# Hybrid attention, feed-forward and selective-scan kernel: the scan's per-tile work for the next tile in a new order, and three edits where stages meet

## The chip, the cores and the metric

The kernel runs on one core of a Trainium2 chip. The metric is the device time of one execution in microseconds (us). Three executions of the kernel before took 1989.69, 1992.88 and 1998.08 us; the median is 1992.88 us. The core's engines work side by side, each through its own list of instructions in order: TensorE (PE, with its weight loads as PEld), VectorE (DVE), ScalarE (ACT), GpSimd (POOL) and SyncE (SP), which issues the DMAs. They wait for each other by semaphores.

## What is computed

x is (4, 1024, 256) in float32, 4096 tokens. Four blocks follow each other, each on the layer-normed x and added to x:

```python
x = x + attn_a(_layernorm(x))   # 16 heads, latent q and kv, rotary part, softmax over 1024 keys
x = x + ffn(_layernorm(x))      # square(relu(x W_fc)) W_proj, 5 spiking steps
x = x + attn_b(_layernorm(x))   # selective scan, below
x = x + ffn(_layernorm(x))
```

The part that most of the change is in:

```python
x_res, z, params = x @ W_x.T, x @ W_z.T, x @ W_params.T
dt = softplus(params[..., :64] @ W_dt.T + b_dt)        # (b, l, 256)
u = silu(conv4(x_res))                                 # depthwise, 4 taps, causal
A = -exp(A_log)                                        # (256, 16)
h = exp(dt*A)*h + (exp(dt*A)-1)/A * B_t * u_t          # 16 states a channel, over l
y = sum_n C_t[n]*h[n] + u*D_param
out = (y * silu(z)) @ W_out.T
```

## The kernel before, in words

A tile is 512 tokens; there are NT = 8 tiles, two to a sequence (TPB = 2). DC = 2 halves f of 128 channels lie on the partitions. The stages are `project` (latents, rotary parts, and the first 24 pairs of score maxima), `attend`, `merge_heads`, `feed_forward`, `scan`, `feed_forward`. Each stage is a block: the engines meet at its end.

`scan` goes through UNITS = 8 x 16 units g = 16 t + n, one for each tile t and state n. For a unit:

- POOL multiplies u by B (`make_input`, L1672), three units ahead, into a ring of 6 buffers.
- ACT makes the decays exp(dt A) into one of two PSUM buffers `a_bank`, half by half (`make_decay`, L1912). The buffer is free when DVE has scanned unit g-2, and also weighed it where DVE weighs.
- DVE, for each half, forms (a-1)*x (`scale`, L2015) and runs the recurrence over the 512 tokens (`run`, L2024).
- The result is multiplied by C (`weigh`) into one of OUTS = 5 buffers `outs`. POOL does it (L1680) except in the states of the tuple ON_DVE, where DVE does (L2032, one unit later). A buffer of `outs` is free when TensorE has summed unit g-5.
- TensorE sums the unit into `ys_bank` (`unit_sum`, L1744), which needs the weighed unit. Unit 0 of a tile needs the two `ys_bank` free, that is, the tile before gated.

In between, in an order written out by hand and told by n, stands the work for the next tile and the end of the last one. TensorE, at its step n, first does what is written for n and then sums unit n-3. For tile t+1 it makes the parameters (`parameters`), the products for dt (`step_size`, one a half), the convolved input (`u_taps`, two taps at a time), and it adds four parts of softplus by matmuls with the identity (`add_terms`). For tile t it makes z (`z_half`) and the output product (`out`, in two halves of 256 tokens). All of these share two PSUM banks, w0 and w1. ACT empties the banks: `keep_par`, `soft_split` (Abs and Relu), `soft_exp`, `soft_log`, `soft_rest`, `silu_u`, `keep_step` (which writes dt), `silu_z`. [...] DVE multiplies y by silu(z) after state 2 of the next tile (`gate`, L1992) and adds the output product to x (`add`, L1996); before, the two adds stand after state 3 and are those of tile t-2.

TensorE, ACT and DVE each take what is written in their own order: a wait in TensorE's list holds up every sum behind it, and by OUTS the weighing of later units.

## Time and profile before

| | |
|---|---|
| median of three runs | 1992.88 us |
| profiled execution | 1992.94 us, its span 1991.2 us |
| TensorE busy in the span | 1885.0 us (95%) |
| VectorE busy | 1611.4 us (81%) |
| ScalarE busy | 1100.8 us (55%) |
| GpSimd busy | 682.3 us (34%) |
| `project` and its 24 pairs | 0 to about 168 us |
| `attend` | about 168 to 917 us |
| `merge_heads` | about 917 to 955 us |
| first `feed_forward` | about 955 to 1208 us |
| `scan` | about 1208 to 1762 us |
| second `feed_forward` | about 1762 to 1991 us |

Times in the rows are us from the start of the span. A row of the timeline merges equal instructions that follow each other and gives their common time; in brackets stands how long the engine was idle before and what ended that. A float32 matmul stands as two instructions in the trace. The profiled execution is 1.7 us longer than its span.

### The profile page before, as it was taken

The numbers are of one execution on the slowest core, as the hardware profiler recorded it, in microseconds if no ns is written. First come the engines' busy times: TensorE is split into PE (matmuls) and PEld (weight loads), VectorE is DVE, ScalarE is ACT, GpSimd is POOL, SyncE is SP. The second block draws the span as 40 slices with busy tenths as digits, with TensorE's granted clock in tenths as the row PEclk, the third lists the DMA queues.
The fourth block names the chain that finished last, engine by engine and source line by source line (L and its number), as shares of the span: only waits on it lengthen the run. The fifth ranks groups of instructions, "written<-read, shape, count | busy, mean of one in ns | idle before, by whom it ended". The sixth has DMA issues, their size and how long they took to land. (4 is left out here: it accounts for less than half of the span.)

```text
span 1991.2 us, 26035 instructions
## 1 busy us (share of the span) xinstructions
PE 1885.0 (95%) x7526; PEld 845.0 (42%) x7526; DVE 1611.4 (81%) x2582; ACT 1100.8 (55%) x1526; POOL 682.3 (34%) x467
## 2 busy tenths in 40 slices
PE   8989999999999999999999997899999999699998
PEld 4532332332322323324676663343344344256666
DVE  6888998998999989985556658999998999954655
ACT  5643666665666666673234345776578558333322
POOL 3651000110100000010000017999999999800000
PEclk9997999998999999999999998999999999899999
DMA  4661222221221222204210023545444555400000
GB/s 136 163 155 33 44 44 45 44 49 39 49 44 44 49 44 44 44 12 143 65 43 32 11 56 102 135 136 143 143 132 124 135 129 164 94 6 16 22 21 22
DMA packets 100426, 147.14 MB, mean 74 GB/s; under 512 B 15120, under 2 KB 54432, under 8 KB 98752
## 3 DMA queue, kind: packets, MB, share of 16 engines
q1 hardware_dynamic: 100288, 145.42, 28.7%
q8 instruction: 72, 1.18, 0.3%
q14 instruction: 66, 0.54, 0.1%
HBM read 114.69 MB, written 30.29 MB: 73 GB/s over the span
## 5 line engine op out<-in xcount | busy, mean ns | idle before, releaser
L888 DVE TENSOR_REDUCE mx<-max_bank 128x1 f32<-128x512 f32 x976 | 627.9, 686 | 61.0 <-PE max_bank L791 59.9
L874 ACT ACTIVATE probs<-score_bank 128x1024 f32<-128x1024 f32 x512 | 496.7, 1021 | 277.0 <-PE score_bank L805 276.2
L791 PE MATMUL max_bank<-ks,qs 96*128 96x512 bf16 x976 | 338.9, 388 | 0.0
L805 PE MATMUL score_bank<-qs,ks 99*128 99x512 bf16 x1024 | 311.9, 386 | 12.9 <-issue 9.9
L1672 POOL TENSOR_TENSOR ring<-u,bc 128x1024 f32<-128x1024 f32 x128 | 301.2, 2367 | 0.0
L1744 PE MATMUL ys_bank<-outs,rec_diag 128*128 128x512 f32 x512 | 249.3, 616 | 46.2 <-POOL outs L1680 22.1
L858 PE MATMUL o_bank<-probs,vg 128*32 128x512 f32 x2048 | 273.6, 606 | 0.1
L1680 POOL TENSOR_TENSOR outs<-ring,bc 128x1024 f32<-128x1024 f32 x95 | 224.4, 2362 | 26.6 <-DVE ring L2024 26.3
L1312 PE MATMUL y_bank_f<-wpr_f,hid_f 128*128 128x256 f32 x992 | 229.9, 379 | 0.0
L1912 ACT ACTIVATE a_bank<-dt,decay_s 128x512 f32<-128x512 f32 x256 | 169.4, 684 | 109.1 <-DVE ring L2024 64.9
L745 POOL CAST neg_parts<-neg_max 16x128 bf16<-16x128 f32 x31 | 8.7, 281 | 639.8 <-DVE neg_max L901 639.8
L791 PEld LDWEIGHTS max_bank<-ks,qs 96*128 96x128 bf16 x976 | 95.4, 98 | 283.0 <-DVE mx L888 187.8
L1312 PEld LDWEIGHTS y_bank_f<-wpr_f,hid_f 128*128 128x128 f32 x992 | 187.3, 190 | 60.2 <-issue 39.5
L2015 DVE SCALAR_TENSOR_TENSOR ring<-a_bank,ring 128x512 f32<-128x512 f32 x256 | 171.1, 669 | 34.9 <-ACT a_bank L1912 34.9
L1744 PEld LDWEIGHTS ys_bank<-outs,rec_diag 128*128 128x128 f32 x512 | 96.6, 194 | 173.8 <-issue 125.0
L805 PEld LDWEIGHTS score_bank<-qs,ks 99*128 99x128 bf16 x1024 | 99.4, 100 | 117.4 <-issue 21.7
L2024 DVE TENSOR_TENSOR_SCAN ring<-a_bank,state,ring 128x512 f32<-128x512 f32 x94 | 119.4, 1271 | 0.0
L1303 PE MATMUL hid_bank_f<-xn_f,wfc_f 128*128 128x512 f32 x256 | 116.5, 592 | 1.0 <-PEq L1023 1.0
L2024 DVE TENSOR_TENSOR_SCAN ring<-a_bank,ring 128x512 f32<-128x512 f32 x96 | 116.2, 1210 | 0.0
L1401 ACT ACTIVATE relu_f<-a_bank 128x512 f32<-128x512 f32 x64 | 38.1, 597 | 137.4 <-PE a_bank L1303 113.5
L1711 PE MATMUL work<-xn_s,wtap_s 128*128 128x512 f32 x224 | 102.6, 601 | 0.0
L1303 PE MATMUL a_bank<-xn_f,wtap_s 128*128 128x512 f32 x224 | 101.8, 592 | 0.0
(256 smaller groups left out, 2043.5 us busy)
## 6 DMA issues: line engine op xcount, KB each, us to landing
bc<-bc_scr SPq DMA_DIRECT2D x128, 512.0 KB, 4.9
qk_parts<-parts SPq DMA_DIRECT2D x128, 96.0 KB, 1.9
qs<-qk_parts SPq DMA_DIRECT2D x128, 64.0 KB, 4.2
o_scr<-o_sb SPq DMA_DIRECT2D x32, 256.0 KB, 2.1
ks<-qk_parts SPq DMA_DIRECT2D x16, 384.0 KB, 4.6
xn_s<-xn_scr SPq DMA_DIRECT2D x8, 515.0 KB, 6.3
x<-in_x_dram SPq DMA_DIRECT2D x8, 512.0 KB, 4.1
ks<-qk_parts SPq DMA_DIRECT2D x16, 256.0 KB, 3.7
```

The costliest lines, as they stand in the source:

```text
L791: nc.tensor.matmul(max_bank[(r + a) % MB][:], qs[r][0:SROWS, half, j, qt * P:(qt + 1) * P], ks[r][0:SROWS, j, kh * TW:(kh + 1) * TW], star ...
L805: mm = nc.tensor.matmul(score_bank[pair][:, j % 2], ks[r][0:MROWS, j, kt * P:(kt + 1) * P], qs[r][0:MROWS, qh, j, :], start=True, stop=True)
L858: mm = nc.tensor.matmul(o_bank[32 * j:32 * j + 32, :], vg[r][:, kt, j], probs[:, s % 2, j], start=(kt == 0), stop=(kt == QT - 1))
L874: nc.scalar.activation(probs[:, s % 2, 2 * pair:2 * pair + 2], score_bank[pair][:], ACT.Exp, scale=SOFTMAX_SCALE).then_inc(probs_ready, 1)
L888: nc.vector.tensor_reduce(mx[:, a // HU, a % HU:a % HU + 1], max_bank[(r + a) % MB][:], AX_X, ALU.max)\
L1303: mm = nc.tensor.matmul(hid_bank[f % BANKS], wfc[:, c, f * P:(f + 1) * P], xn_of(t, c), start=(c == 0), stop=(c == DC - 1))
L1312: mm = nc.tensor.matmul(y_of(t, b), hid[:, f, b * P:(b + 1) * P], wpr[:, f], start=(f == 0), stop=(f == FC - 1))
L1672: nc.gpsimd.tensor_tensor(ring[:, g % RING], u[t % 2][:], bc[:, g % BC, 0:1].to_broadcast([P, DC, TW]), ALU.mult).then_inc(inputs, 1)
L1680: nc.gpsimd.tensor_tensor(outs[:, g % OUTS], ring[:, g % RING], bc[:, g % BC, 1:2].to_broadcast([P, DC, TW]), ALU.mult).then_inc(weighted, 1)
L1744: mm = nc.tensor.matmul(y_bank[f][:], rec_diag[:, f * NS + n], outs[:, g % OUTS, f], start=(n == 0), stop=(n == NS - 1))
L2015: nc.vector.scalar_tensor_tensor(x, a, 1.0, x, ALU.subtract, ALU.mult).then_inc(scaled, 1)
L2024: nc.vector.tensor_tensor_scan(a if on_dve(g) else x, a, x, state[:, f, n:n + 1] if t % TPB else 0.0, ALU.mult, ALU.add)\
```

## The change

There are three places.

**Project to attend.** TensorE gets products whose result nobody reads (`keep_warm`): 4 before the first of the 24 pairs of score maxima, 8 before the second, 2 before each of the others.

**Merge of the heads.** SyncE issues the loads of head tile 3 ahead of the wait for the reciprocals, and the three small reciprocal loads only ahead of tile 5.

**Scan.** The work for the next tile is laid out anew. The two halves of dt stay in two banks (w0, w1), `soft_exp`, `soft_log`, the four silus and the two `keep_step` come in pairs, so that a tile has six table loads. The states that DVE weighs are 0, 5, 9 and 12 (before 3, 7, 11, 15). The output product and the adds of tile t-1 stand in tile t (before: those of t-2), its adds after DVE's states 5 and 7. At the end, both first hidden products of the next stage stand before the last two sums.

```diff
+            def keep_warm(products):
+                for _ in range(products):
+                    nc.tensor.matmul(lat_bank[:], begun["qs0"][0:SROWS, 0, 0, 0:P], begun["ks0"][0:SROWS, 0, 0:TW],
+                                     start=True, stop=True)
+            keep_warm(4)
             for n in range(FIRST_PAIRS):
+                if n == 1:
+                    keep_warm(8)
+                elif n:
+                    keep_warm(2)
...
+            sp.wait_ge(divided, DC)
+            load_heads(sp, by_rows, o_in, LOADED, heads_in[0])
             sp.wait_ge(recip_split, 5)
...
-    ON_DVE, ON_DVE_LAST = (3, 7, 11, 15), (3, 6, 9, 12, 15)
+    ON_DVE, ON_DVE_LAST = (0, 5, 9, 12), (3, 6, 9, 12, 15)
...
@@ TensorE's order in scan @@
-                    if t >= TPB and n == 1:
-                        pe.wait_ge(soft_made, DC * (t + 1))
-                        out(t - 2, 0, w0)
-                    if t >= TPB and n == 2:
+                    if more and n == 3:
+                        parameters(t + 1)
+                    if t and n == 3:
                         pe.wait_ge(z_kept, DC * t)
-                        out(t - 2, 1, w1)
+                        out(t - 1, 0, w1)
+                    if more and n == 5:
+                        pe.wait_ge(par_kept, t + 2)
+                        step_size(t + 1, 0, w0[:])
+                    if t and n == 5:
+                        pe.wait_ge(x_new, 2 * t - 1)
+                        out(t - 1, 1, w1)
                     if more:
-                        if n == 4:
-                            parameters(t + 1)
-                            if t >= TPB:
-                                pe.wait_ge(x_new, DC * (t - 1))
-                            pe.wait_ge(z_kept, DC * t)
-                            u_taps(t + 1, 0, (0, 1), w1[:])
-                        if n == 5:
-                            u_taps(t + 1, 0, (2, 3), w1[:])
-                        if n == 6:
-                            pe.wait_ge(par_kept, t + 2)
-                            step_size(t + 1, 0, w0[:])
+                        if n == 7:
+                            if t:
+                                pe.wait_ge(x_new, 2 * t)
+                            step_size(t + 1, 1, w1[:])
+                            pe.wait_ge(split, SPLIT * (t + 1) + 2)
+                            u_taps(t + 1, 0, (0, 1), w0[:])
                         if n == 8:
-                            pe.wait_ge(split, SPLIT * (t + 1) + 2)
-                            step_size(t + 1, 1, w0[:])
+                            u_taps(t + 1, 0, (2, 3), w0[:])
                         if n == 9:
-                            pe.wait_ge(u_kept, DC * (t + 1) + 1)
+                            pe.wait_ge(split, SPLIT * (t + 1) + 4)
                             u_taps(t + 1, 1, (0, 1), w1[:])
                         if n == 10:
                             u_taps(t + 1, 1, (2, 3), w1[:])
                         if n == 12:
-                            add_terms(t + 1, 0)
+                            add_terms(t + 1, 0, w0[:])
+                            add_terms(t + 1, 1, w1[:])
                         if n == 14:
-                            add_terms(t + 1, 1)
+                            pe.wait_ge(soft_made, DC * (t + 1) + 1)
+                            z_half(t, 0, w0[:])
+                            pe.wait_ge(soft_made, DC * (t + 2))
+                            z_half(t, 1, w1[:])
...
@@ ScalarE's order @@
-                    if t and n == 0:
+                    if t and n == 1:
+                        silu_z(t - 1, 0, w0[:])
                         silu_z(t - 1, 1, w1[:])
                         exp_tables()
...
+                        if n == 13:
+                            silu_u(t + 1, 0, w0[:])
                             silu_u(t + 1, 1, w1[:])
                             exp_tables()
                         if n == 15:
-                            keep_step(t + 1, 1)
+                            keep_step(t + 1, 0, w0[:])
+                            keep_step(t + 1, 1, w1[:])
...
@@ VectorE's order @@
-                        if t >= TPB and n == 3:
-                            add(t - 2, 0, w0)
-                            add(t - 2, 1, w1)
+                        if t and n == 5:
+                            add(t - 1, 0, w1)
+                        if t and n == 7:
                             add(t - 1, 1, w1)
```

TensorE's list where a tile of the scan meets the next. Here `ys_bank` rows are the sums (x2 is one unit, x10 five), `wpar_s` the parameters, `wtap_s` two taps of the convolved input, `par,wdt_s` the product for dt, `wout_s,gy` half of the output product. Before:

```order
L1744 MATMUL ys_bank<-outs,rec_diag 128x512 x4
L1733 MATMUL work<-wout_s,gy 128x256 x4
L1744 MATMUL ys_bank<-outs,rec_diag 128x512 x2
L1733 MATMUL work<-wout_s,gy 128x256 x4
L1744 MATMUL ys_bank<-outs,rec_diag 128x512 x4
L1696 MATMUL work<-xn_s,wpar_s 96x512 x2
L1711 MATMUL work<-xn_s,wtap_s 128x512 x4
L1744 MATMUL ys_bank<-outs,rec_diag 128x512 x2
L1711 MATMUL work<-xn_s,wtap_s 128x512 x4
L1744 MATMUL ys_bank<-outs,rec_diag 128x512 x2
L1696 MATMUL work<-par,wdt_s 128x512
```

The same place in the changed kernel:

```order
L1761 MATMUL ys_bank<-outs,rec_diag 128x512 x10
L1715 MATMUL work<-xn_s,wpar_s 96x512 x2
L1750 MATMUL work<-wout_s,gy 128x256 x4
L1761 MATMUL ys_bank<-outs,rec_diag 128x512 x4
L1715 MATMUL work<-par,wdt_s 128x512
L1750 MATMUL work<-wout_s,gy 128x256 x4
L1761 MATMUL ys_bank<-outs,rec_diag 128x512 x4
L1715 MATMUL work<-par,wdt_s 128x512
L1728 MATMUL work<-xn_s,wtap_s 128x512 x4
L1761 MATMUL ys_bank<-outs,rec_diag 128x512 x2
L1728 MATMUL work<-xn_s,wtap_s 128x512 x4
L1761 MATMUL ys_bank<-outs,rec_diag 128x512 x2
```

The last three units and the first of the next tile are no longer parted by output products; both halves of the output product now stand behind the gate, and the taps begin behind the second `par,wdt_s` product.

ScalarE's list from the second half of u on, before (`dt<-work` is `keep_step`, `sz` is silu(z), the `a_bank` rows are the decays):

```order
L1849 ACT_TABLE_LOAD
L1849 ACTIVATE u<-work 128x512
L1859 ACT_TABLE_LOAD
L1926 ACTIVATE state<-a_bank 128x2
L1912 ACTIVATE a_bank<-dt,decay_s 128x512 x2
L1898 ACTIVATE dt<-work 128x512
L1912 ACTIVATE a_bank<-dt,decay_s 128x512 x2
L1926 ACTIVATE state<-ring 128x2
L1856 ACT_TABLE_LOAD
L1856 ACTIVATE sz<-work 128x512
L1859 ACT_TABLE_LOAD
```

And in the changed kernel:

```order
L1860 ACT_TABLE_LOAD
L1860 ACTIVATE u<-work 128x512 x2
L1870 ACT_TABLE_LOAD
L1920 ACTIVATE a_bank<-dt,decay_s 128x512 x4
L1906 ACTIVATE dt<-work 128x512 x2
L1920 ACTIVATE a_bank<-dt,decay_s 128x512 x4
L1867 ACT_TABLE_LOAD
```

Both copies of dt now stand behind the decays of state 15, directly ahead of those of the next tile's state 0, and both halves of silu(z) behind state 1 of the next tile.

## Rows read from the trace of the kernel before

**Rows 1.** The costliest groups of the scan: instruction, shapes, count, busy us, mean ns, idle before.

```profile
L1744 PE MATMUL ys_bank<-outs,rec_diag 128*128 128x512 f32 x512 | 249.3, 616 | 46.2 <-POOL outs L1680 22.1 <-DVE gy L1992 22.0 <-DVE outs L2032 2.1
L1680 POOL TENSOR_TENSOR outs<-ring,bc 128x1024 f32<-128x1024 f32 x95 | 224.4, 2362 | 26.6 <-DVE ring L2024 26.3
L2015 DVE SCALAR_TENSOR_TENSOR ring<-a_bank,ring 128x512 f32<-128x512 f32 x256 | 171.1, 669 | 34.9 <-ACT a_bank L1912 34.9
```

**Rows 2.** TensorE's timeline behind gates: start, us, instruction, count, idle before.

```profile
1286.86 3.49 PE L1744 MATMUL ys_bank<-outs,rec_diag 128*128 128x512 f32 x4 [5.32 <-DVE gy L1992]
...
1351.93 1.98 PE L1744 MATMUL ys_bank<-outs,rec_diag 128*128 128x512 f32 x4 [2.41 <-DVE gy L1992]
...
1418.59 2.79 PE L1744 MATMUL ys_bank<-outs,rec_diag 128*128 128x512 f32 x4 [3.15 <-DVE gy L1992]
1422.84 3.70 PE L1696 MATMUL work<-xn_s,wpar_s 128*96 128x512 f32 x4 [1.46 <-DVE x L1996]
...
1691.13 3.70 PE L1744 MATMUL ys_bank<-outs,rec_diag 128*128 128x512 f32 x8 [3.14 <-DVE gy L1992]
```

**Rows 3.** VectorE's timeline in tile 1 and at the start of tile 2.

```profile
1287.32 1.28 DVE L2024 TENSOR_TENSOR_SCAN a_bank<-a_bank,state,ring 128x512 f32<-128x512 f32 x1
...
1289.10 1.27 DVE L2024 TENSOR_TENSOR_SCAN a_bank<-a_bank,state,ring 128x512 f32<-128x512 f32 x1
...
1350.62 1.26 DVE L1992 TENSOR_TENSOR gy<-ys_bank,sz 128x512 f32<-128x512 f32 x2
...
1352.39 1.22 DVE L2024 TENSOR_TENSOR_SCAN a_bank<-a_bank,ring 128x512 f32<-128x512 f32 x1
...
1354.11 1.21 DVE L2024 TENSOR_TENSOR_SCAN a_bank<-a_bank,ring 128x512 f32<-128x512 f32 x1
1355.24 1.26 DVE L1996 TENSOR_TENSOR x<-work,x 128x512 f32<-128x512 f32 x2
...
1357.02 1.21 DVE L2032 TENSOR_TENSOR outs<-a_bank,bc 128x1024 f32<-128x1024 f32 x1
1358.15 1.21 DVE L2024 TENSOR_TENSOR_SCAN ring<-a_bank,ring 128x512 f32<-128x512 f32 x1
```

**Rows 4.** TensorE's timeline in the middle of tile 2.

```profile
1372.90 1.12 PE L1696 MATMUL work<-par,wdt_s 64*128 64x512 f32 x2
1373.95 1.98 PE L1744 MATMUL ys_bank<-outs,rec_diag 128*128 128x512 f32 x4
1375.77 3.60 PE L1711 MATMUL work<-xn_s,wtap_s 128*128 128x512 f32 x8
1379.21 1.88 PE L1744 MATMUL ys_bank<-outs,rec_diag 128*128 128x512 f32 x4
```

**Rows 5.** Waits of the scan: engine, waited for, us in total, times, longest.

```profile
DVE ring L2015 <- ACT a_bank L1912: 34.9, 24, 4.3
ACT e_part L1868 <- PE work L1696: 33.3, 7, 5.9
```

**Rows 6.** Timelines of ScalarE and VectorE at the softplus logarithm of tile 0.

```profile
1251.23 1.28 ACT L1859 ACT_TABLE_LOAD   x1
...
1253.25 0.69 DVE L2015 SCALAR_TENSOR_TENSOR ring<-a_bank,ring 128x512 f32<-128x512 f32 x1 [1.84 <-ACT a_bank L1912]
```

**Rows 7.** From project to attend: busy us in two stretches, and TensorE's timeline.

```profile
core 0: us, PE busy (x) PEld busy (x) DVE busy (x) ACT busy (x) POOL busy (x), PEclk, DMA share, GB/s
140.00:168.00 28.00, 21.83 (x44) 2.90 (x45) 26.32 (x24) 0.63 (x1) 4.48 (x9) 0.50 0.19 42
168.00:175.00 7.00, 7.00 (x23) 2.18 (x23) 4.21 (x7) 4.09 (x4) 4.97 (x4) 0.59 0.00 0
...
142.74 1.04 PE L378 MATMUL comp_banks<-ks,qs 96*128 96x512 bf16 x2 [0.19 <-DVE row_max L511]
```

**Rows 8.** TensorE's timeline in the merge, and behind the scan's last sum.

```profile
930.19 3.72 PE L1085 MATMUL out_bank<-wo,o_n 128*128 128x256 f32 x16
...
1755.01 1.88 PE L1818 MATMUL a_bank<-xn_s,wtap_s 128*128 128x512 f32 x4
```

More of the change, by code:

```diff
@@ L1052, in _ @@
                 .then_inc(recips_out, 16)
-            sp.wait_ge(recips_out, 16)
-            for part in range(3):
-                sp.dma_start(recip_heads[part * H:(part + 1) * H, B - 1], recip_scr[part, HEADS0:]).then_inc(recips_in, 16)
-            for t in range(LOADED, NT):
+            for t in range(LOADED + 1, NT):
+                if t == LOADED + 2:
+                    sp.wait_ge(recips_out, 16)
+                    for part in range(3):
+                        sp.dma_start(recip_heads[part * H:(part + 1) * H, B - 1], recip_scr[part, HEADS0:])\
+                            .then_inc(recips_in, 16)
                 sp.wait_ge(divided, DC * (t - LOADED) + DC)
@@ L1717, in step_size, with add_terms @@
                 product(bank, [(wdt[:, f * P:(f + 1) * P], par[0:R])], dt_made)
-            def add_terms(t, f):
+            def add_terms(t, f, bank):
                 pe.wait_ge(rest_made, 2 * t)
-                pe.wait_ge(split, SPLIT * t + 7 + f)
-                if f:
-                    pe.wait_ge(soft_made, DC * t + f)
-                product(w0[:], [(ident[:], part[:, f]) for part in (e_part, rest_part, log_part, relu_part)], terms_added)
+                pe.wait_ge(split, SPLIT * t + 8)
+                pe.wait_ge(u_kept, DC * t + f + 1)
+                product(bank, [(ident[:], part[:, f]) for part in (e_part, rest_part, log_part, relu_part)], terms_added)
             def z_half(t, f, bank):
@@ L1970, in _ @@
                             norm.scale(nc, act, 0, 0)
-                        if n == 11:
-                            norm.keep(nc, act, 0, (w0, w1), xn_next)
-                    if n == 14:
-                        silu_z(t, 0, w1[:])
-                        exp_tables()
-                    if not more and n == 15:
-                        silu_z(t, 1, w1[:])
-                        exp_tables()
+                        if n == 10:
+                            silu_z(t, 0, w0[:])
+                            silu_z(t, 1, w1[:])
+                            exp_tables()
+                        if n == 12:
+                            norm.keep(nc, act, 0, (w0, w1), xn_next)
             keep_state(UNITS - 2)
@@ L2052, in tiles @@
                             gate(t - 1)
-                        if t >= TPB and n == 3:
-                            add(t - 2, 0, w0)
-                            add(t - 2, 1, w1)
-                        if not more and n == 5:
-                            add(t - 1, 0, w0)
-                        if not more and n == 6:
+                        if t and n == 5:
+                            add(t - 1, 0, w1)
+                        if t and n == 7:
                             add(t - 1, 1, w1)
```

74 lines of the change are left out of this document (28 added, 46 removed).

## The prediction

> **What bounds the kernel now.** I read the page's busy times first, then the waits and groups of the scan, and then the timelines of the four engines from gate to gate, because the change is almost all there. In the costliest groups [rows 1] three engines are each close to full: TensorE's sums stood idle only 46.2 us in a scan of some 550, GpSimd waited for VectorE 26.6 us in all, and VectorE for ScalarE's decays 34.9 us. No engine has room for a new wait. What repeats is the way from one gate to the next. TensorE's first sum behind a gate starts at 1286.86 for tile 0 and at 1691.13 for tile 6 [rows 2]: 404.3 us for six tiles, 67.4 a tile (65.1 the first; 67.8 to 68.4 from the second full gate on). The reader is to see in rows 2 to 4 what one such way is made of.
>
> **VectorE's and TensorE's prices.** Half a state (one product and one scan) takes VectorE 1287.32 to 1289.10 = 1.78 us in an odd tile and 1352.39 to 1354.11 = 1.72 in an even one, a gate 1.2 (1.26 with overlap), an add 0.6, a weighing 1357.02 to 1358.15 = 1.13 [rows 3]. TensorE at full clock takes 1375.77 to 1379.21 = 3.44 us for 8 float32 instructions of 512 columns, that is 0.43 each, and 1372.90 to 1373.95 = 1.05 for a product for dt [rows 4]. A unit's sum is four of them, 1.72.
>
> **The scan, tiles 1 to 6: the new wait.** The table loads that go (ten to six a tile, 1.28 each [rows 6]) relieve ScalarE; the wait of ScalarE for the product for dt (33.3 us, 7 times, and with it the longest stalls of VectorE [rows 5]) should go too, since that product now stands three states ahead of its reader. What comes in their place is in TensorE's list: the second product for dt, all taps and all sums from unit 4 on stand behind the second add of the tile before, and VectorE does that add only after its state 7. Let G be the end of a gate and A the end of that add.
>
> G to A on VectorE: states 3 to 7 are ten halves, 17.8 us in odd tiles and 17.2 in even ones; the weighing of state 5 is 1.13; two adds 0.6 + 0.7. Sum 20.2 and 19.6. TensorE has little to do there: two halves of the output product, four sums and one product for dt, some 11.6 us, and it stands idle for about 8.5.
>
> A to the last sum on TensorE: 32 instructions of taps, 48 for the sums of units 4 to 15, 4 for the D term, 16 for the added terms, 8 for z. That is 108 x 0.43 = 46.4, and 1.05 for the product for dt: 47.5, with 0.4 for the latencies at its waits 47.9. All of this is one list in order, and none of it can move ahead of A. Then the gate, 1.2.
>
> Sum: 20.2 + 47.9 + 1.2 = 69.3 us in odd tiles, 68.7 in even ones, 69.0 in the mean, against 67.4 now. This is nearly a floor: only the clock and the latencies are estimates in it.
>
> On top comes state 0's new weighing on VectorE: it needs the sum of the unit five before (unit 11), which now stands behind both halves of z, 6.9 us (16 x 0.43) ahead of TensorE's end. Behind it VectorE still has the weighing, 1.13, one scan, 1.2, and three halves, 5.3, to the gate: 7.6. So the gate is 0.7 later: 69.7. And the clock: behind a gate with idle times of 3.15 and 1.46 us the four instructions for the parameters took 3.70 us at 1422.84 where two of them at full clock would end in 1.05 [rows 2, 4], a loss of about 1.8. The new way has three idle times of that kind ahead of A (estimates 2.8, 1.8 and 3.5), but what runs slowly ahead of A costs nothing; only a clock that is still low behind A does. I take 0.3 for it and keep 0 and 1.9 as ends. 70.0 a tile; six tiles 420.0, +15.7 on the 404.3.
>
> Rows and a page point the same way about such idle times: the Trainium skill (TensorE: Matmul & The Clock Gate, "HAM oscillation — how this bites in real kernels") says that waits between bursts of matmuls throttle the clock again and again. By that, each of the six tiles would lose 1.9 more, 2019 in all; the traces show such losses behind gates of 3.1 us idle only, hence the small value.
>
> **Tile 0** has no add to wait for. Its taps now wait for `soft_split` behind the decays of state 8. VectorE's product for state 11 comes at 1253.25, of which 1.84 is stall [rows 6]; 7 halves (12.0), one weighing (1.13) and a small stall (0.3) back from 1251.4, state 6 ended at 1238.0; with two weighings ahead of it instead of one it is 1239.1; decays and two splits add about 1.9. From 1241 on TensorE has 46.4 + 0.4, and VectorE ends 0.7 later: gate from 1288.5, its end at 1289.7 instead of 1286.8. +2.8; ends 0 and 4.
>
> **ScalarE's pairs.** A pair with its two loads is 3.7 to 3.8 us in one piece where the logarithm's 3.95 now stalls VectorE for 1.84 [rows 6]. One such stall (state 11) stays, those of the silus fall beside weighings. Either way they end ahead of the wait for TensorE and cost nothing; were that cover gone, they would cost some 2 us a tile.
>
> **Last tile.** VectorE has two adds less in it (-1.2). Behind it, 3.4 us of hidden products (two times 1.88 less overlap [rows 8]) move from beside and behind the last gate to ahead of the last two sums; the next stage starts with VectorE's last add, which comes about 0.8 later. Together 0, ends -2 and +2.
>
> **Project to attend.** In the 28 us of the 24 pairs VectorE is busy for 26.32 [rows 7], so 1.7 us is all that faster matmuls can give there; I take 1.0. The next 7 us run at a mean clock of 0.59: at most 2.9 more if the clock stays up, but between the pairs and `attend` TensorE stands idle for about 3 us either way, after which [rows 2] the clock fell: 0.5. Together -1.5, ends -4.6 and, if the clock falls in spite of the products, a loss: a pair's two matmuls take 1.04 at low clock [rows 7], four would take some 1.75 against 1.18 a pair now, 24 x 0.6 = +14. I hold that for unlikely (1 in 20): no row of such a stretch at low clock and without idle time is there to show it.
>
> **Merge.** TensorE works without a break there, 3.7 us a tile [rows 8], while VectorE waits for head tiles; the earlier load is hidden by TensorE. 0. If the loads delayed the sums' load by more than about 3 us, TensorE would wait; ends 0 and +2.
>
> **Sum.** 1992.9 (profiled execution, 1.7 over its span; the median of the runs is the same) - 1.5 + 2.8 + 15.7 + 0 + 0 = 2009.9: 2010 us. Its low end: six tiles at 68.9 (+9.1), tile 0 and last tile at 0 and -1, passages -3: 1998. Its high end: six tiles at 71.6 (+25.3), tile 0 +2.8, and +1 elsewhere: 2022.
>
> **Rivals.**
> 1. The order does what a lighter ScalarE would suggest: the stalls of VectorE go and TensorE never holds anything up. Then GpSimd is the bound and its 26.6 us of waiting go: 1992.9 - 26.6 - 1.5 = 1965. For it: 34.9 us of VectorE's stalls are ScalarE's and the longest are TensorE's lateness, mended here. Against it: it needs A to G in 43 us on TensorE, and the count gives 47.9. 0.04. The Trainium skill (ScalarE: Activation LUTs, "Table sets: the hidden batching unit") wants activations batched by table set, which is what the pairs do; four loads less a tile at the row's 1.28 us are 36 us of ScalarE in seven tiles, and by that rule alone the time would end where GpSimd stops it, at this rival's 1965.
> 2. VectorE's own way is the bound, 16 states, four weighings, adds and gate, 63.5, and one stall of 1.9: 65.4 a tile, as if the adds came early enough: 1992.9 - 1.5 + 2.8 - 12 = 1982. Same reason against it. 0.04.
> 3. The new wait is there and costs as in the low end, since something I count twice (latencies, the state-0 weighing) is not there: 1996 to 2002, slower by under 0.5%. 0.18.
> 4. As forecast, 2003 to 2018. 0.60.
> 5. The low clock reaches behind A in every tile, or the dummy products run at low clock: 2019 to 2026. 0.14.
>
> A measurement tells 0.5%, 10 us, from no change. Slower by more than that: cases 4 and 5 and a little of 3, 0.75; within: most of 3, half of 2, 0.19; faster 0.06. The range 1998 to 2022 leaves out the two faster cases and part of 5, under 2 in 10.
>
> **What the changed profile would show.** Gates 69 to 71 us apart in tiles 1 to 6. TensorE idle for 3 us or more ahead of the second product for dt, released by VectorE's add (L1999), and nearly none from there to the last sum. VectorE stalled on the decays of the next tile's state 0 for about 2 us, on its weighing of state 0 (by the sum) for 1 to 2, and at or near the gate by TensorE. GpSimd waiting more than now. ScalarE's wait ahead of Abs small. The clock near 1 from 139 to 165 us. The forecast is wrong if the gates are under 68 us apart, or if TensorE is not idle ahead of that add.

## The result, and the profile after

The changed kernel takes 2004.2 us (median of 10 runs, 1996.6 to 2012.9) against 1993.7 for the kernel before on the same chip (1986.1 to 2000.2): ratio 1.0058, interval 1.0038 to 1.0077, slower by 7.6 to 15.4 us. Forecast were 2010 us and "slower". The profiled execution of the changed kernel is its fastest run, 1996.6 us with a span of 1994.8. One of the four executions of the kernel with earlier splits (below) took 2770.9 us at a granted clock of 0.65, and its numbers leave that one out.

The two spans differ by only 3.6 us, but their parts differ by more. GpSimd's first instruction of the scan starts at 1208.29 before and at 1194.93 after; from there to the last gate it is 546.9 us before and 565.0 after; from the last gate to the second `feed_forward` 7.2 and 6.1. So in these two executions the scan is 17.0 us longer, and what lies ahead of it 13.4 us shorter. Sections further down show that most of those 13.4 are not the change's.

**The gates.** Starts of the gates on VectorE, from their rows in the timeline, tile 0 to tile 7:

| | 0 | 1 | 2 | 3 | 4 | 5 | 6 | 7 |
|---|---|---|---|---|---|---|---|---|
| before | 1285.54 | 1350.62 | 1417.27 | 1485.11 | 1553.46 | 1621.47 | 1689.82 | 1755.21 |
| after | 1275.13 | 1344.91 | 1416.02 | 1487.49 | 1556.90 | 1626.68 | 1695.24 | 1759.90 |
| way, before | | 65.1 | 66.7 | 67.8 | 68.4 | 68.0 | 68.4 | 65.4 |
| way, after | | 69.8 | 71.1 | 71.5 | 69.4 | 69.8 | 68.6 | 64.7 |

Six ways from gate to gate take 404.3 us before and 420.1 after: +15.8. Tile 0, from GpSimd's first instruction, takes 77.25 and 80.20: +2.95. The last tile is 0.7 shorter, the tail behind it 1.1.

**One way from gate to gate after, on TensorE.** The timeline of tile 2 (what answers to rows 2 and 4; columns as there):

```profile
1346.32 1.97 PE L1750 MATMUL work<-wout_s,gy 128*128 128x256 f32 x8 [0.41 <-DVE gy L1995]
1348.12 3.60 PE L1761 MATMUL ys_bank<-outs,rec_diag 128*128 128x512 f32 x8
1354.42 1.12 PE L1715 MATMUL work<-par,wdt_s 64*128 64x512 f32 x2 [2.70 <-ACT par L1853]
1357.11 3.60 PE L1750 MATMUL work<-wout_s,gy 128*128 128x256 f32 x8 [1.57 <-DVE x L1999]
1360.55 3.60 PE L1761 MATMUL ys_bank<-outs,rec_diag 128*128 128x512 f32 x8
1365.75 1.12 PE L1715 MATMUL work<-par,wdt_s 64*128 64x512 f32 x2 [1.61 <-DVE x L1999]
1366.81 5.40 PE L1728 MATMUL work<-xn_s,wtap_s 128*128 128x512 f32 x8
1372.04 1.88 PE L1761 MATMUL ys_bank<-outs,rec_diag 128*128 128x512 f32 x4
1373.76 3.60 PE L1728 MATMUL work<-xn_s,wtap_s 128*128 128x512 f32 x8
...
1402.94 3.60 PE L1715 MATMUL work<-xn_s,wz_s 128*128 128x512 f32 x8
1406.38 8.75 PE L1761 MATMUL ys_bank<-outs,rec_diag 128*128 128x512 f32 x20
1414.96 1.88 PE L1715 MATMUL work<-xn_s,wpar_s 128*96 128x512 f32 x4
```

There are four brackets ahead of 1366 and none behind. TensorE waits 6.3 us while it holds little work, starts the second product for dt the moment VectorE's add has ended, and then works without a break until its last sum ends at 1414.96. The first eight taps took 5.40 where the next eight took 3.60, 1.8 us lost to the clock. Two windows of the changed kernel show that it was not a low clock left over from ahead of the add (the granted clock is the third number from the right):

```profile
1360.50:1366.80 6.30, 4.69 (x11) 1.65 (x10) 6.30 (x9) 3.93 (x8) 6.30 (x4) 1.00 0.60 162
1366.80:1370.20 3.40, 3.40 (x6) 1.50 (x6) 3.40 (x5) 1.72 (x4) 3.40 (x3) 0.56 0.49 130
```

It was low in the output's second half (3.60 for what takes 1.97), full in the two sums, and fell anew as the taps began, behind waits of 2.70, 1.57 and 1.61.

**The same way on VectorE** (what answers to rows 3):

```profile
1344.91 1.26 DVE L1995 TENSOR_TENSOR gy<-ys_bank,sz 128x512 f32<-128x512 f32 x2
...
1356.38 0.67 DVE L1999 TENSOR_TENSOR x<-work,x 128x512 f32<-128x512 f32 x1
...
1357.57 1.21 DVE L2035 TENSOR_TENSOR outs<-a_bank,bc 128x1024 f32<-128x1024 f32 x1
...
1365.04 0.66 DVE L1999 TENSOR_TENSOR x<-work,x 128x512 f32<-128x512 f32 x1
...
1389.48 1.22 DVE L2035 TENSOR_TENSOR outs<-a_bank,bc 128x1024 f32<-128x1024 f32 x1 [2.11 <-PE ys_bank L1761]
...
1400.92 0.69 DVE L2018 SCALAR_TENSOR_TENSOR ring<-a_bank,ring 128x512 f32<-128x512 f32 x1 [2.17 <-ACT a_bank L1920]
...
1408.37 1.23 DVE L2035 TENSOR_TENSOR outs<-a_bank,bc 128x1024 f32<-128x1024 f32 x1 [1.48 <-PE ys_bank L1761]
...
1416.02 1.26 DVE L1995 TENSOR_TENSOR gy<-ys_bank,sz 128x512 f32<-128x512 f32 x2
```

The reader is to see two halves: up to the second add (ends 1365.70) VectorE never waits and TensorE does; behind it VectorE waits in five places, for TensorE's sums or for decays, and TensorE never does. Each engine is idle while it is the other's turn. That is what a single ordered list with one wait in it makes of two nearly full engines.

**All tiles**, by the starts and ends of those rows (G the gate's end, A the second add's end):

| tile | G to A | A to the last sum's end | from there to the gate | way |
|---|---|---|---|---|
| 1 | 20.1 | 47.6 | 0.9 | 69.8 |
| 2 | 19.5 | 49.3 | 1.1 | 71.1 |
| 3 | 20.1 | 49.3 | 0.9 | 71.5 |
| 4 | 19.5 | 47.6 | 1.1 | 69.4 |
| 5 | 20.1 | 47.6 | 0.9 | 69.8 |

With the gate's 1.26 each row adds up to its way. Tile 6 (68.6) hands over to the last tile, which has another order.

**The groups and the waits.** Answers to rows 1 and 5, first the groups, then the waits (us in total, times, longest):

```profile
L1761 PE MATMUL ys_bank<-outs,rec_diag 128*128 128x512 f32 x512 | 241.6, 613 | 12.8 <-DVE outs L2035 7.4 <-POOL outs L1699 5.4
L1699 POOL TENSOR_TENSOR outs<-ring,bc 128x1024 f32<-128x1024 f32 x95 | 223.6, 2353 | 42.9 <-DVE ring L2027 22.2 <-PE ys_bank L1761 20.6
L2018 DVE SCALAR_TENSOR_TENSOR ring<-a_bank,ring 128x512 f32<-128x512 f32 x256 | 171.3, 669 | 29.6 <-ACT a_bank L1920 29.6
```

```profile
ACT dt L1906 <- PE work L1715: 30.9, 13, 2.8
...
PE work L1715 <- ACT par L1853: 22.1, 7, 5.4
...
DVE outs L2035 <- PE ys_bank L1761: 20.2, 14, 2.3
...
PE work L1750 <- DVE x L1999: 15.8, 7, 8.5
...
PE work L1715 <- DVE x L1999: 7.0, 6, 1.7
```

ScalarE's wait for the product for dt at the Abs (33.3 us, 7 times [rows 5]) is gone, but its wait at the copies of dt is 30.9 where it was 9.5 before. TensorE's sums hardly wait any more (12.8 us against 46.2 [rows 1], 22 of which were for gates), yet the scan is longer: the idle time moved from the sums to the rows ahead of the add. GpSimd waits 42.9 us where it waited 26.6, half of it now for TensorE.

**The passages.** Windows of the changed kernel from project to attend (answer to rows 7; the granted clock is the third number from the right), and TensorE's timeline at the merge's first products (rows 8):

```profile
140.00:168.00 28.00, 22.65 (x86) 6.92 (x85) 24.78 (x25) 2.05 (x2) 5.04 (x10) 0.96 0.13 28
168.00:175.00 7.00, 7.00 (x36) 2.15 (x35) 6.26 (x11) 4.11 (x5) 2.19 (x1) 0.92 0.00 0
```

```profile
908.17 3.72 PE L1103 MATMUL out_bank<-wo,o_n 128*128 128x256 f32 x16
912.36 3.72 PE L1103 MATMUL out_bank<-wo,o_n 128*128 128x256 f32 x16
```

The granted clock is 0.96 where it was 0.50, as it should be, and the merge's first tile takes 3.72 us.

### The profile page after: what moved, and what is told of

The parts are those of the page before. It is cut to its first block and busy times, and to the rows that moved or that the text cites. A ratio compares the mean times of both kernels' runs of the same rounds, so it can differ in the third digit from the quotient of the medians.

```text
span 1994.8 us, 26113 instructions
## 1 busy us (share of the span) xinstructions
PE 1888.5 (95%) x7582; PEld 856.2 (43%) x7582; DVE 1611.0 (81%) x2582; ACT 1061.1 (53%) x1482; POOL 682.5 (34%) x467
## 5 line engine op out<-in xcount | busy, mean ns | idle before, releaser
L818 PE MATMUL score_bank<-qs,ks 99*128 99x512 bf16 x1024 | 307.4, 382 | 13.0 <-issue 9.6
L1761 PE MATMUL ys_bank<-outs,rec_diag 128*128 128x512 f32 x512 | 241.6, 613 | 12.8 <-DVE outs L2035 7.4
L1699 POOL TENSOR_TENSOR outs<-ring,bc 128x1024 f32<-128x1024 f32 x95 | 223.6, 2353 | 42.9 <-DVE ring L2027 22.2
L1761 PEld LDWEIGHTS ys_bank<-outs,rec_diag 128*128 128x128 f32 x512 | 101.1, 199 | 137.4 <-issue 124.5
L818 PEld LDWEIGHTS score_bank<-qs,ks 99*128 99x128 bf16 x1024 | 98.5, 99 | 114.4 <-issue 17.1
```

The costliest lines, as they stand in the source:

```text
L818: mm = nc.tensor.matmul(score_bank[pair][:, j % 2], ks[r][0:MROWS, j, kt * P:(kt + 1) * P], qs[r][0:MROWS, qh, j, :], start=True, stop=True)
L1699: nc.gpsimd.tensor_tensor(outs[:, g % OUTS], ring[:, g % RING], bc[:, g % BC, 1:2].to_broadcast([P, DC, TW]), ALU.mult).then_inc(weighted, 1)
L1761: mm = nc.tensor.matmul(y_bank[f][:], rec_diag[:, f * NS + n], outs[:, g % OUTS, f], start=(n == 0), stop=(n == NS - 1))
```

## The experiments

All are compared with the kernel before on the same chip. "The scan" is, in each one's profile, the time from GpSimd's first instruction of it to the first product of the second `feed_forward`: 554.1 us before (1208.29 to 1762.39), 571.1 after (1194.93 to 1766.02). It is a finer measure of an edit inside it than the median, and an experiment's verdict on the scan goes by it and by the gates.

### The scan alone, and the passages alone

The kernel before with the changed scan and nothing else; and the kernel before with the two passages changed and its own scan. Both edits are the hunks of the diff ahead of the prediction.

> The changed kernel's scan with project, attend and merge as before. If the time is lost where the prediction said (gates 70.0 us apart in tiles 1 to 6 instead of 67.4, tile 0 2.8 longer), the scan takes 17 us more than before and the whole 2010 to 2011. If the scan's loss were less in most runs than in the two traces, 2000 to 2005.

Measured: 2014.1 us, ratio 1.0106 (1.008 to 1.0132), +21 us with an interval of 16 to 26. The gates are 69.8, 71.1, 71.5, 69.4, 69.8, 68.6 and 64.7 us apart, the changed kernel's to 0.02 us. So the scan's 17 us are its own and don't depend on what ran ahead of it. Its merge belongs to the order before and shows what that can cost:

```profile
934.13 0.60 PE L1075 MATMUL spread_bank<-recip_heads,head_parts 48*128 48x512 bf16 x2 [1.99 <-DVE o_n L569]
934.66 5.41 PE L1085 MATMUL out_bank<-wo,o_n 128*128 128x256 f32 x16
...
932.79 1.28 DVE L569 TENSOR_TENSOR o_n<-o_in,spread_bank 128x512 f32<-128x512 f32 x2 [4.11 <-DMA o_in<-o_scr]
```

VectorE waits 4.1 us for a head tile, so TensorE stands idle for 2.0, and its next tile runs at low clock: 5.41 instead of 3.72.

> The kernel before with the two edits outside the scan alone (the products that keep TensorE busy between project and attend, and SyncE's order in the merge). The prediction's count: 1.5 us less than before, 1992. The two traces so far say more: the changed kernel reached the scan 13.3 us earlier, of which 3.0 lie ahead of attend, 1.0 in its first steps, 5.6 in attend and 2.9 in the merge, where the clock was low in the one trace (0.52 in 7 us) and not in the other. Theory A (the passages give some 4 us, the rest is chance of the clock in attend): 1988 to 1991. Theory B (the products also spare attend low-clock stretches, and SyncE's order or they spare the merge its own): 1983 to 1987, with the clock at 1.0 at the merge's start in this trace too. Rival: nothing, 1993.

Measured: 1991.1 us (12 runs), ratio 0.9978 (0.9961 to 0.9994): -4.4 us, interval -7.8 to -1.2, which still holds the forecast's -1.5. The scan is as before (gates 65.4 to 68.7 apart).

### The two passages apart

The dummy products alone:

```diff
+            pe.wait_ge(latent_kept, 2 * NT)
             pe.wait_ge(stack_in, 2 * STACK_LOAD)
+            keep_warm(4)
...
+                if n == 1:
+                    keep_warm(8)
+                elif n:
+                    keep_warm(2)
```

> The kernel before with only the products that keep TensorE's clock up from project to attend; the merge and the scan are as before. The two passages together gave -4.4 us (ratio 0.9978). Theory (most of that is the merge, where the stage took 35.8 us with the edit and 39.6 in one profile and 37.0 in another without it): the 24 pairs stay 1.13 us apart as VectorE sets them, attend's first sums start 1 to 2 us earlier, and the time falls by 1.5 us. Rival (the products do most of it): the time falls by 3.5 us or more. Second rival: the clock of attend's later stretches changes with them, then the profile shows it in a row of windows after 175 us and the time moves by up to 6.

Measured: 1994.3 us (12 runs), ratio 1.0003 (0.9987 to 1.0019): nothing, at most -2.6 us. The clock is up as intended, and it buys little because VectorE's 24 reductions, back to back at 1.13 us, set the pace of the pairs. From the first of them to attend's first score product it is 30.0 us in the three profiles without these products and 29.3 in the eleven with them: 0.7 us, which the time of the whole can't show. The windows as above:

```profile
140.00:168.00 28.00, 22.57 (x88) 6.91 (x89) 25.38 (x24) 1.15 (x2) 5.81 (x11) 0.99 0.18 40
168.00:175.00 7.00, 7.00 (x31) 2.28 (x33) 5.96 (x10) 4.74 (x6) 3.95 (x2) 0.78 0.00 0
```

SyncE's order in the merge alone:

```diff
+            sp.wait_ge(divided, DC)
+            load_heads(sp, by_rows, o_in, LOADED, heads_in[0])
             sp.wait_ge(recip_split, 5)
...
-            for t in range(LOADED, NT):
+            for t in range(LOADED + 1, NT):
+                if t == LOADED + 2:
+                    sp.wait_ge(recips_out, 16)
```

> The kernel before with only SyncE's new order in the merge (the next head tile's load ahead of the rest of the reciprocals' way, the three loads of the reciprocals one tile later). Theory: VectorE's wait for the third head tile goes (4.1 us in the scan-only kernel's profile, with TensorE idle 2 us and slow for the next 5.4), from first out_bank to ffn1 35 to 36 us against 37 to 39.6, time -2 to -3 us. Rival (my forecast's term: TensorE hides the load, 0): no change, 36.5 to 37 us from out_bank to ffn1.

Measured: 1992.0 us (12 runs), ratio 0.9981 (0.9965 to 0.9998): -3.8 us, interval -7.0 to -0.4. As far as the intervals tell, this is most of the passages' gain. Before, a head tile is late for VectorE; with the new order none is. VectorE's row in the merge of the kernel before:

```profile
932.55 1.28 DVE L569 TENSOR_TENSOR o_n<-o_in,spread_bank 128x512 f32<-128x512 f32 x2 [2.10 <-DMA o_in<-o_scr]
```

And TensorE and VectorE in the merge of the kernel with the new order alone (the last row is the start of the first turned tile):

```profile
921.69 3.72 PE L1090 MATMUL out_bank<-wo,o_n 128*128 128x256 f32 x16
...
930.42 1.29 DVE L569 TENSOR_TENSOR o_n<-o_in,spread_bank 128x512 f32<-128x512 f32 x2
...
950.36 1.04 PE L1008 MATMUL turn_bank_mh<-ident_s,scaled_x_mh 128*128 128x128 f32 x8
```

From the first output product to the first turned tile it is 28.7 us here and 28.7 to 30.4 in the eleven profiles with this order (29.0 in the changed kernel), 29.3 in the mean; in the three without it, 31.5 (before), 32.5 and 34.1: 3.4 between the means. This has two parts. VectorE waits for a head tile in all three profiles without the edit and in none of the eleven with it; that wait cost TensorE nothing in the kernel before, 0.9 us in the kernel with the dummy products alone, and 3.7 with the scan alone (2.0 idle, 1.7 of low clock). The rest is the first tile, which ran at low clock in all three without the edit (5.4 to 6.5 us) and in four of the eleven with it (5.1 to 5.4); that this hangs on the order was not shown, and may be chance.

### The add later, and earlier

If the wait for VectorE's second add sets the way, one state more ahead of it must show in full. Changed kernel, the adds one state later:

```diff
-                        if t and n == 5:
+                        if t and n == 6:
                             add(t - 1, 0, w1)
-                        if t and n == 7:
+                        if t and n == 8:
                             add(t - 1, 1, w1)
```

> The changed kernel with VectorE's two adds one state later (after states 6 and 8 instead of 5 and 7), nothing else. If the second add sets when TensorE's 47.9 us begin, every gate of tiles 1 to 6 comes 3.4 to 3.6 us later: 73.5 apart, and with up to 2 us in the last tile the time is 21 to 23 us over the changed kernel's, 2026. If VectorE's own way or GpSimd set the gates, the adds' place is free and the time stays at 2004.

Measured: 2021.9 us, ratio 1.0134 (1.0106 to 1.0162). Six ways of 73.3, 73.4, 73.3, 73.4, 73.3 and 72.6 us: 439.3 in all against 420.1, 3.2 a tile for one state of 3.5; G to A is 23.6 and 23.0, A to the last sum 47.6 to 48.1. The last tile is 2.2 us shorter than in the changed kernel, so the scan is 17.1 longer and the median 17.7 where 21 to 23 were expected. The wait ahead of the output's second half grows from 1.57 to 6.19:

```profile
1373.33 3.78 PE L1750 MATMUL work<-wout_s,gy 128*128 128x256 f32 x8 [6.19 <-DVE x L1999]
```

Then the other way: adds behind states 3 and 4, and with them the second half of the output product, both products for dt and ScalarE's pieces one or two places up:

```diff
-                        if t and n == 5:
+                        if t and n == 3:
                             add(t - 1, 0, w1)
-                        if t and n == 7:
+                        if t and n == 4:
                             add(t - 1, 1, w1)
...
-                    if t and n == 5:
+                    if t and n == 4:
                         pe.wait_ge(x_new, 2 * t - 1)
                         out(t - 1, 1, w1)
...
-                        if n == 7:
+                        if n == 6:
                             if t:
                                 pe.wait_ge(x_new, 2 * t)
                             step_size(t + 1, 1, w1[:])
...
-                        if n == 6:
+                        if n == 5:
                             keep_par(t + 1)
-                        if n == 8:
+                        if n == 7:
                             soft_split(t + 1, 0, w0[:])
-                        if n == 10:
+                        if n == 9:
                             soft_split(t + 1, 1, w1[:])
```

> The changed kernel with the adds after states 3 and 4, the second half of the output product at TensorE's step 4, the second product for dt at step 6, and keep_par and the two soft_split one state earlier (5, 7, 9), so that the taps begin some 6 us earlier. If the wait for the second add is the cause, TensorE's way from gate to gate falls to 64 us, and VectorE's own (65.4 by the prediction, with stalls 66) takes over: 4 us a tile less than the changed kernel, some 24 to 27 us in all, 1978. If the cause is another (ScalarE's pairs, state 0's weighing), at most 1 us a tile, 1998 to 2004.

Measured: 1981.2 us, ratio 0.9933 (0.9912 to 0.9954): 23 us better than the changed kernel, and better than the one before. The ways are 65.4, 65.3, 65.4, 66.6, 65.4 and 64.5; the scan is 545.3. The rest of the changed scan (paired logarithms and silus, each pair with one table load ahead of it and one behind, six a tile; states 0, 5, 9, 12) stayed, so its dear places were among the pieces moved here. Which of them is the next question.

### The adds alone

Is the add the only wait? Changed kernel with the adds behind states 3 and 4 and the output's second half one place up, all else where the change put it.

> The changed kernel with only the two adds moved, to behind states 3 and 4 (and with them the second half of the output product, one place up in TensorE's list); both products for dt, the taps, ScalarE's pieces and the tail stay where the change put them. Theory (what holds TensorE back is the add of state 7, nothing else): the way from gate to gate is VectorE's own, 64.4 to 66.6 us as with all pieces moved, six tiles 393 instead of 420, time 1980 to 1983. Rival (the second product for dt and its split, still behind state 7, are a second wait of nearly the same length: VectorE's state 7 no longer holds it, but ScalarE's split behind state 8 does): gates 67 to 69, six tiles 408, time 1992.

Measured: 1998.2 us (10 runs), ratio 1.0017 (1.0003 to 1.0031). The rival holds, though the ways are 69.4, 68.7, 68.7, 68.5, 70.1 and 67.8, 413.1 in all, 5 more than it had: 7 us of the 28 that the early kernel gains in six tiles. TensorE's timeline in tile 3:

```profile
1424.49 1.99 PE L1750 MATMUL work<-wout_s,gy 128*128 128x256 f32 x8 [0.37 <-DVE x L1999]
...
1429.29 1.12 PE L1715 MATMUL work<-par,wdt_s 64*128 64x512 f32 x2 [1.09 <-ACT par L1853]
...
1433.97 1.12 PE L1715 MATMUL work<-par,wdt_s 64*128 64x512 f32 x2
1438.79 5.26 PE L1728 MATMUL work<-xn_s,wtap_s 128*128 128x512 f32 x8 [3.70 <-ACT relu_part L1878]
```

The wait for the add is down to 0.37, but the taps now wait 3.70 for ScalarE's split, which stands behind the decays of state 8, and start at low clock in all six tiles (5.2 to 6.7 us for eight). A second wait lay right behind the first, and in the changed kernel nothing showed it, because the first ended later. The split moved alone, without the add, was not run. In the early kernel (with the tail of before, below) that row reads:

```profile
1434.44 3.70 PE L1728 MATMUL work<-xn_s,wtap_s 128*128 128x512 f32 x8 [2.36 <-ACT relu_part L1877]
```

### The tail

The early kernel's last tile took 68.1 us, its gate waiting for TensorE:

```profile
1739.37 3.67 PE L1761 MATMUL ys_bank<-outs,rec_diag 128*128 128x512 f32 x4 [3.40 <-POOL outs L1699]
1742.87 3.60 PE L1828 MATMUL a_bank<-xn_s,wtap_s 128*128 128x512 f32 x8
1746.31 3.59 PE L1761 MATMUL ys_bank<-outs,rec_diag 128*128 128x512 f32 x8
```

Behind a wait of 3.40 four instructions took 3.67 (1.88 at full clock), and then the next stage's products stand ahead of the last two sums. With the tail of the kernel before:

```diff
-                if g == UNITS - 2:
-                    ...
-                    next_hidden(0)
-                    next_hidden(1)
                 unit_sum(g)
+            ...
+            next_hidden(0)
             out(NT - 1, 0, w0)
             out(NT - 1, 1, w1)
+            next_hidden(1)
```

> The kernel with the adds after states 3 and 4 (1981.2), and behind its last sum the order of the kernel before: both next stage's hidden products behind the sums again, one ahead of and one behind the last outs. Theory: the last gate no longer waits 5.3 us for TensorE; the last tile takes 65 to 66 us instead of 68.1, but 3.4 us of hidden products come partly behind it, of which before's own tail hid all but about 1: 1979, -2 us. Rival (the wait was for the sums, the products fill idle time): no change or +1. If the low clock of that tail goes with it, 1977.

Measured: 1976.8 us, ratio 0.991 (0.9887 to 0.9933). Last tile 64.8 instead of 68.1, from the gate to the next stage 7.2 instead of 6.1: 2.2 us less together, as expected. But the scan is 545.7 against 545.3: in this profile the taps of tiles 1 and 2 ran at low clock and their ways are 66.5 instead of 65.4 and 65.3. So the 4 us between the medians can't be put down to the tail; 2 of them may be.

### Which states VectorE weighs

```diff
-    ON_DVE, ON_DVE_LAST = (0, 5, 9, 12), (3, 6, 9, 12, 15)
+    ON_DVE, ON_DVE_LAST = (3, 7, 11, 15), (3, 6, 9, 12, 15)
```

> The changed kernel with VectorE weighing states 3, 7, 11 and 15 again instead of 0, 5, 9, 12; nothing else. The weighing of state 15 then waits for the sum of unit 10, which stands ahead of both halves of z, so it comes some 7 us earlier in TensorE's list than the one state 0's waited for. Theory (my term of 0.7 a tile for state 0's weighing, and 1.1 in tile 0): gates 69.1 us apart in the mean instead of 70.0, six tiles 415 to 416, tile 0 1.1 less, time 1999, -5 us. Rival (TensorE's list alone sets the gate): gates 70.0 apart, time 2004. Second rival (GpSimd's units in new places hold up TensorE's sums): gates 71, 2010.

Measured: 2006.1 us, ratio 1.0056 (1.0036 to 1.0077), as the changed kernel. The ways are 69.5, 69.3, 69.8, 69.3, 69.5 and 69.8: 417.2 in six, 2.9 less; tile 0 is 0.4 shorter (1.1 expected) and the last tile is 67.5, 2.8 more, so the rival on the time is right and the theory on the tiles half right. The gate comes 0.6 to 1.0 us behind the last sum, against 0.9 to 1.1 with state 0: its weighing is worth 0.2 us a tile, not 0.7. The clock gives 3.4: no tile had slow taps behind the add, where the changed kernel had two. Against both stands the sixth way, which is 1.3 longer (69.8 for 68.6). The taps in the third way:

```profile
1445.52 1.12 PE L1715 MATMUL work<-par,wdt_s 64*128 64x512 f32 x2
1446.57 3.70 PE L1728 MATMUL work<-xn_s,wtap_s 128*128 128x512 f32 x8
```

The same swap on the early kernel with the old tail:

> The kernel with early adds and the tail of before (1976.8), VectorE weighing states 3, 7, 11, 15. In the changed kernel that swap gave 2.9 us in six tiles and cost 2.8 in the last one. Theory (state 0's weighing costs only what stands behind TensorE's late sums, and here VectorE is the bound): gates move by less than 0.4 us each, the last tile is 1 to 3 us longer: 1977 to 1979. Rival (states 0, 5, 9, 12 are the worse places also here): gates 65.0 in every tile, 1973.

Measured: 1974.4 us, ratio 0.9898 (0.9867 to 0.9929). The ways are 65.9 and 65.7 in turn, the last tile 63.8, 1.0 shorter where 1 to 3 longer was expected, tile 0 1.3 longer, and the scan is 546.0 against 545.7 without the swap: the same. What differs between the two medians, 2.4 us, lies ahead of it.

### ScalarE's splits one state earlier

```diff
-                        if n == 7:
+                        if n == 6:
                             soft_split(t + 1, 0, w0[:])
-                        if n == 9:
+                        if n == 8:
                             soft_split(t + 1, 1, w1[:])
```

> The kernel with early adds and the tail of before, ScalarE's two splits one state earlier each (behind the decays of states 6 and 8 instead of 7 and 9). In its profile TensorE stands idle 2.36 us a tile for the split ahead of the first taps, and its clock is low behind that in three of six tiles (5.3 to 5.4 us for 8 taps instead of 3.7). Theory: that wait goes, the clock stays up, the gates of 66.5 become 65.4 and the time falls by 3 to 4 us: 1973. Rival (VectorE is the bound and waits for no tap): no change, 1976 to 1977.

Measured: 1974.1 us (three runs), ratio 0.9894 (0.9856 to 0.9931); but the scan takes 548.6 us, 2.9 more than without the edit. The wait of 2.36 ahead of the taps is gone, and in all six tiles a longer one, 2.8 to 3.1 us, stands further down the list; behind it the clock was low for several products in two of them (ways of 67.1 and 68.4). Here is the second:

```profile
1515.30 2.05 PE L1715 MATMUL work<-e_part,ident_s 128*128 128x512 f32 x2 [3.11 <-ACT u L1859]
1517.13 1.91 PE L1715 MATMUL work<-xn_out_sb,ident_s 128*128 128x512 f32 x2
```

TensorE came to the added terms sooner than ScalarE's silu, waited 3.1 us and ran them at low clock (2.05 and 1.91 for what takes 1.02). The six ways are 1.2 us longer together than without the edit, and tile 0 is 1.6 longer. Idle time ahead of the taps was a little cheaper. My expectation of -3 to -4 us failed for the scan, and by the median alone one would have taken it for nearly met.

> Both of the last two steps at once: early adds, tail of before, states 3, 7, 11, 15 on VectorE, and ScalarE's splits one state earlier. Apart they gave 1974.4 (gates 65.7 to 65.9 in every tile) and 1974.8 (65.3 where the clock held, 67.1 and 68.4 in two tiles where it did not). Theory (with the clock up VectorE alone sets the gate, 63.5 us of its own and 2.4 of waits for ScalarE's decays, and the splits only move TensorE's idle time): gates 65.7 to 65.9, time 1974, no change against either. Rival (they add up): gates 65.0, 1970. Second rival (the splits' earlier place makes ScalarE late for a decay ahead of them): gates 66.5, 1978.

Measured: 1978.7 us, ratio 0.992 (0.9896 to 0.9945), the scan 547.2, ways 65.7 to 66.5. No gain over either, as the theory had it; but its ways of up to 66.5 and its time fit the second rival's 66.5 and 1978 as well, and the two were not told apart. The four kernels with the old tail stand at 1974 to 1979 us with overlapping intervals, their scans at 545.7 to 548.6; no run here tells which is best, only that each is 15 to 21 us faster than the kernel before.

## Why the prediction was right, and where it was off

**The new wait (forecast: G to A 20.2 and 19.6, A to the last sum 47.9, gate 1.2).** Right, and shown: 20.1 and 19.5, 47.6, 1.26. Moving the add by a state moved the way by 3.2 us, and taking it and the split behind it off the path gave 65.4, the number that rival 2 had for that case. That the second product for dt, the taps and most sums stand behind one add in one list sets the way in this kernel; the split would set nearly the same way without it (68.8 against 70.0).

**State 0's weighing (0.7) and the clock (0.3).** Their sum, 1.0 a tile, is right only by compensation. From the list's end to the gate I had 0.4 of latencies and 0.7 for the weighing; measured are 0.9 to 1.1, of which 0.6 to 1.0 stay when the weighing is elsewhere. So it was worth 0.2. The clock cost 1.7 in two tiles of six, 0.6 in the mean, twice the value taken and inside its bounds of 0 and 1.9; and it was not the "clock that is still low behind A" that I had priced, but one that was full ahead of A and fell again behind it. The sixth way, which hands over to the last tile, had no term of its own and is 1.1 shorter than the 69.7 it was given. Six tiles: 420.0 forecast, 420.1 measured; agreement that close is luck, since these errors of -1.1 to +1.4 a tile cancel.

**What the changed profile was to show.** Neither sign of a wrong forecast came: the gates are at least 68.6 us apart, and TensorE is idle ahead of the add. But "idle for 3 us or more ahead of the second product for dt" is not met: 0.5 to 1.7 us there. TensorE was idle for 6.3 us ahead of A rather than the 8.5 worked out, since the low clock stretched the work between the waits (3.60 for the output's second half, 1.97 for the first), and 2.7 of it came at the first product for dt, for ScalarE's copy of the parameters. The slack was the same, its place another. What I missed there is the second wait: I named what would be late next on GpSimd and VectorE but not ScalarE's split, which holds the way at 68.8 us in the mean when the add no longer does.

**Tile 0.** +2.8 forecast, +2.95 measured.

**Last tile and tail.** 0 forecast with ends of -2 and +2, -1.8 measured. The two adds less are in it (-0.7 net), the tail is 1.1 shorter.

**Project to attend.** -1.5 forecast; the dummy products alone gave +0.6, interval -2.6 to +3.8. The bound of 1.7 us on the pairs from VectorE's share in rows 7 was the useful part. In the stretch itself they gain 0.7 us in every profile, half of what was forecast.

**Merge.** 0 forecast with ends 0 and +2, -3.8 measured (interval -7.0 to -0.4). This is the step that failed: "the earlier load is hidden by TensorE". I had looked at TensorE's unbroken run of products [rows 8] in one profile; in it VectorE waited 2.1 us for the third head tile (the row above), and TensorE was only just not reached. A margin that small turned over in the two other kernels with the old order (0.9 us; and 4.1 of waiting, 2.0 idle, 1.7 more of low clock), and I had excluded a gain though a row of VectorE's spoke for one. What those waits cost is 1.5 us in the mean of the three; how much of the rest of the 3.8 is the order's stays open.

**The sum.** With the merge at -3.8, the products at 0 and the scan at +17.0, the sum from 1992.9 is 2006.1 against 2010 forecast and 2004.2 measured. The 13.4 us that the changed kernel's profile is ahead at the scan's start are thus mostly not the change: 2.9 lie ahead of attend (0.7 of them the dummy products'), 2.5 in the merge and 8.0 in attend, where all kernels run the same instructions. From its first score product to the merge's first output product it is 755.4 us in the kernel with the merge's order alone, 751.1 before and 743.1 after, and the windows from 175 to 900 us of these three, in that order, show why:

```profile
175.00:900.00 725.00, 713.88 (x3944) 214.41 (x3945) 651.36 (x1060) 475.92 (x491) 71.15 (x155) 0.98 0.21 43
```

```profile
175.00:900.00 725.00, 714.86 (x3972) 214.43 (x3968) 652.74 (x1064) 479.20 (x495) 71.20 (x155) 0.99 0.21 44
```

```profile
175.00:900.00 725.00, 715.21 (x4004) 213.23 (x4002) 654.05 (x1063) 485.37 (x502) 71.56 (x156) 1.00 0.21 46
```

The granted clock (third number from the right) rises from 0.98 to 1.00, and with it the work done in the same 725 us (3944 to 4004 matmuls). It differs between executions of like code, and is the likely source of the spread of 14 to 16 us between runs of one kernel; that it is all of it was not shown.

## What to carry to other kernels

Where an engine's work is one ordered list, write down for each wait in it what stands behind it and how long that is; releaser's time plus the list behind it is a floor for the period. Here its two terms came within 0.1 and 0.3 us of what was measured (19.9 and 47.9 forecast, 19.8 and 47.6 in the even run of the clock), and the way was 1.0 us above the floor. When such a wait is mended, look for the one that ends just ahead of it: both had to be moved, and the add alone gave 7 us of 28. Judge an edit inside one stage by that stage's own time, since medians of the whole moved by several us for reasons that lay elsewhere, and count an engine "hidden" only with the margin that the row of its neighbour shows.

## What the hardware showed that I had not expected

- The same wait does not always cost clock. TensorE stood idle for 5.0 to 6.3 us in four pieces between gate and add in every tile of the changed kernel, but the taps behind it took 5.40 us in two tiles and 3.70 in the other four; with the adds one state later it was idle for 9.3 to 10.2 us there, and the taps took 3.70 in all six; in the early kernel with the old tail, idle for 2.36 us right ahead of them, 5.3 to 5.4 in three of six. Within one program it is repeatable: two kernels with the same scan and other passages had gates alike to 0.02 us in all tiles.
- With at most 1.1 us ahead of the taps (early adds, states 3, 7, 11, 15 on VectorE) they took 3.70 us in all six tiles, and the ways are even, 65.9 and 65.7.
- Low clock ahead of a wait is free: the output's second half took 3.60 instead of 1.97 us in the changed kernel, and the way from G to A is VectorE's count to 0.1 us.
